# Gate and value products of a local feed-forward as three fp16 products, with the rows split on GpSimd

## The reference, cut to what matters

```python
def _layer(x, wqkv, qs, ksc, wo, lg, lb, w1, b1, w2, b2):
    ...
    x = x + o @ wo                              # window attention
    h = shift_token(x)
    mu = h.mean(-1, keepdims=True)
    var = h.var(-1, keepdims=True)
    h = (h - mu) / jnp.sqrt(var + 1e-05) * lg + lb
    h = h @ w1 + b1                             # 128 -> 2 * 341
    a, g = jnp.split(h, 2, axis=-1)
    h = a * jax.nn.gelu(g, approximate=False)
    x = x + h @ w2 + b2                         # 341 -> 128
    return x
```

## Time and profile before

| | |
|---|---|
| median of three executions | 1896.26 us |
| the profiled execution's own time | 1897.1 us |
| its span, first to last instruction | 1895.3 us |
| TensorE busy | 1763.1 us (93%) |
| VectorE, ScalarE, GpSimd busy | 1410.3, 1421.3, 1426.8 us (74 to 75%) |
| mean granted TensorE clock | 0.963 |
| local layers, first transpose to last write of x | 1300.1 to 1706.5 us |

### The profile page before, as it was taken

One profiled execution on the slowest core, in us unless ns is written; L12 is line 12 of the kernel. 1 busy time (PEld: TensorE's weight loads), 2 busy tenths in 40 slices (PEclk: granted clock), 3 DMA queues, 4 the chain that ended last, 5 costly groups with the idle time before them and its releaser, 6 DMA issues. The chain is left out here.

```text
span 1895.3 us, 54354 instructions
## 1 busy us (share of the span) xinstructions
PE 1763.1 (93%) x23048; PEld 1115.2 (59%) x23048; DVE 1410.3 (74%) x2595; ACT 1421.3 (75%) x1784; POOL 1426.8 (75%) x846
## 2 busy tenths in 40 slices
PE   5999999999999999999999999885999999977997
PEld 1466666666666666666666666582556666642454
DVE  5778878788787878878787776226988888824785
ACT  1688888888888888888888889814888888833463
POOL 3599899999999998998999999974755566504122
PEclk8899999999999999999999999987999999977988
DMA  4101010010101011010110100051211111100000
GB/s 120 26 22 30 19 30 24 25 30 22 27 22 30 24 25 31 19 30 19 31 28 21 27 18 2 2 172 23 44 36 36 37 36 40 28 4 13 1 1 23
DMA packets 71082, 56.91 MB, mean 30 GB/s; under 512 B 29197, under 2 KB 64185, under 8 KB 70841
## 3 DMA queue, kind: packets, MB, share of 16 engines
q1 hardware_dynamic: 70840, 53.44, 11.1%
HBM read 14.54 MB, written 1.05 MB: 8 GB/s over the span
## 5 line engine op out<-in xcount | busy, mean ns | idle before, releaser
L294 POOL TENSOR_TENSOR ah_probs_lo<-ah_probs,ah_probs_hi 128x1024 f16<-128x1024 f32 x512 | 1075.1, 2134 | 106.4 <-ACT ah_probs L493 104.1
L550 DVE TENSOR_REDUCE ah_part_max<-ah_p_m 128x1 f32<-128x512 f32 x1024 | 667.4, 685 | 165.0 <-PE ah_p_m L358 155.7
L490 ACT ACTIVATE ah_probs_hi<-ah_p_s 128x1024 f16<-128x1024 f32 x512 | 529.0, 1033 | 182.7 <-PE ah_p_s L377 176.7
L493 ACT ACTIVATE ah_probs<-ah_p_s 128x1024 f32<-128x1024 f32 x512 | 529.9, 1035 | 0.0
L391 PE MATMUL ah_p_o<-ah_v_hi,ah_probs_hi 128*128 128x65 f16 x4096 | 470.7, 195 | 4.8 <-POOL ah_probs_lo L294 4.6
L393 PE MATMUL ah_p_o<-ah_v_lo,ah_probs_hi 128*128 128x64 f16 x4096 | 470.7, 193 | 0.0
L395 PE MATMUL ah_p_o<-ah_v_hi,ah_probs_lo 128*128 128x65 f16 x4096 | 470.5, 194 | 0.0
L391 PEld LDWEIGHTS ah_p_o<-ah_v_hi,ah_probs_hi 128*128 128x128 f16 x4096 | 383.2, 98 | 86.0 <-DVE a_attn L565 12.3
L393 PEld LDWEIGHTS ah_p_o<-ah_v_lo,ah_probs_hi 128*128 128x128 f16 x4096 | 378.5, 98 | 91.4
L358 PE MATMUL ah_p_m<-ah_k_hi_lo,ah_q_hi_twice 128*128 128x512 f16 x1024 | 394.0, 385 | 6.5 <-DVE ah_part_max L550 5.0
L376 PE MATMUL ah_p_s<-ah_q_hi_twice,ah_k_hi_lo 128*128 128x512 f16 x1024 | 388.7, 380 | 1.1 <-ACT ah_probs L493 0.9
(11 more groups left out here) (279 smaller groups left out, 3100.2 us busy)
## 6 DMA issues: line engine op xcount, KB each, us to landing
ba_v_skew<-ba_v_own SPq DMA_DIRECT2D x64, 129.0 KB, 2.3
ah_q_hi_twice<-ah_hi SPq DMA_DIRECT2D x128, 64.0 KB, 2.0
ah_k_hi_lo<-ah_hi SPq DMA_DIRECT2D x64, 64.0 KB, 1.9
ah_one_k_hi<-ah_hi SPq DMA_DIRECT2D x64, 64.0 KB, 2.0
ah_k_hi_lo<-ah_lo SPq DMA_DIRECT2D x64, 64.0 KB, 2.0
ah_max_q_lo<-ah_lo SPq DMA_DIRECT2D x64, 64.0 KB, 2.0
ah_w_head<-in_w_heads SPq DMA_DIRECT2D x16, 160.0 KB, 2.4
bw_rot<-in_rot SPq DMA_DIRECT2D x4, 512.0 KB, 9.5
```

What stands on the lines that cost most here:

```text
L294: pool.tensor_tensor(pl[:, p % RW, :, :], pb[:, p % RP, :, :], ph[:, p % RW, :, :], ALU.subtract).then_inc(lo_pool, 1)
L490: act.activation(ph[:, p % RW, :, :], p_s[:, p % 2, :, :], ACT.Exp, scale=HD ** -0.5)
L493: act.activation(pb[:, p % RP, :, :], p_s[:, p % 2, :, :], ACT.Exp, scale=HD ** -0.5).then_inc(exp_done, 1)
L550: dve.tensor_reduce(part[:, t, 2 * half + b:2 * half + b + 1], p_m[:, b, :], AX, ALU.max).then_inc(maxed, 1)
```

## The change

The gate and value products, one fp32 product each, become three fp16 products: high weights by high rows, low weights by high rows, high weights by low rows, summed in PSUM. The high part is the fp16 value, the low part the fp16 value of the rest.

The weights `w1` are split on GpSimd in `prepare`, after the rotation tables, from a float32 buffer that now, like that of `wqkv`, is taken by a method `stage` inside `mha_out` and given back at its end. The loads of `w1` have a semaphore of their own.

The rows are split on GpSimd in `local_layers`: in step j, behind the clamp and ahead of the low probabilities, tile u = j-7 of `hT2` is cast to `hT2h` and the rest written to `hT2l`. `hT2` shrinks to two tiles of 128 columns. Gate chunk 0 waits for `hT2l_done` of four tiles in place of `hT2_done`; VectorE's write of `hT2` waits for the split two tiles back in place of `a_ready`.

```diff
@@ mha_out
         aT = sc.sb("attnT", [P, 2, IC, P])
+        local.stage(sc)
@@ LocalWeights
-        self.wqkv = sc.sb("wqkv", [P, DEPTH, 3 * INNER])
...
-        self.w1 = sc.sb("w1", [P, DEPTH, 2 * hid])
+        self.w1h = sc.sb("w1_hi", [P, DEPTH, 2 * hid], F16)
+        self.w1l = sc.sb("w1_lo", [P, DEPTH, 2 * hid], F16)
...
+    def stage(self, sc):
+
+        self.wqkv = sc.sb("wqkv", [P, DEPTH, 3 * INNER])
+        self.w1 = sc.sb("w1", [P, DEPTH, 2 * self.hid])
@@ prepare
+        pool.wait_ge(self.w1_in, 16 * DEPTH)
+        pool.tensor_copy(self.w1h[:, :, :], self.w1[:, :, :]).then_inc(self.w1_hi_done, 1)
+        pool.wait_ge(self.w1_hi_done, 1)
+        pool.tensor_tensor(self.w1l[:, :, :], self.w1[:, :, :], self.w1h[:, :, :],
+                           ALU.subtract).then_inc(self.w1_split, 1)
@@ local_layers, GpSimd, after the clamp
+                    u = j - 7
+                    if on(u):
+                        m, i = divmod(u, GROUP)
+                        ts = slice(i * P, (i + 1) * P)
+                        pool.wait_ge(hT2_done, u + 1)
+                        if m >= 2:
+                            pool.wait_ge(a_ready, HC * (m - 1))
+                        pool.tensor_copy(hT2h[:, m % 2, ts], hT2[:, u % 2, :]).then_inc(hT2h_done, 1)
+                        pool.wait_ge(hT2h_done, u + 1)
+                        pool.tensor_tensor(hT2l[:, m % 2, ts], hT2[:, u % 2, :], hT2h[:, m % 2, ts],
+                                           ALU.subtract).then_inc(hT2l_done, 1)
@@ local_layers, TensorE, gate
-                        pe.wait_ge(hT2_done, GROUP * (m + 1))
+                        pe.wait_ge(hT2l_done, GROUP * (m + 1))
...
-                    pe.matmul(p_h[0:n, :], lw.w1[:, l, col:col + n], hT2[:, m % 2, :], start=True,
+                    cs = slice(col, col + n)
+                    pe.matmul(p_h[0:n, :], lw.w1h[:, l, cs], hT2h[:, m % 2, :], start=True, stop=False)
+                    pe.matmul(p_h[0:n, :], lw.w1l[:, l, cs], hT2h[:, m % 2, :], start=False, stop=False)
+                    pe.matmul(p_h[0:n, :], lw.w1h[:, l, cs], hT2l[:, m % 2, :], start=False,
                               stop=True).then_inc(g_ready if which == 0 else a_ready, 1)
@@ local_layers, VectorE, h2T
-                        if m >= 2:
-                            dve.wait_ge(a_ready, HC * (m - 1))
-                        dve.tensor_scalar(hT2[:, m % 2, i * P:(i + 1) * P], p_e[:, P:2 * P], lw.gb[:, l, 0:1],
+                        if u >= 2:
+                            dve.wait_ge(hT2l_done, u - 1)
+                        dve.tensor_scalar(hT2[:, u % 2, :], p_e[:, P:2 * P], lw.gb[:, l, 0:1],
```

More of the change, by code:

```diff
@@ L802, in __init__ @@
         self.ff_in = sc.long_sem("ff_in")
-        self.FF = 16 * DEPTH * (4 + hc)
+        self.FF = 16 * DEPTH * (3 + hc)
+        self.w1_in, self.w1_hi_done, self.w1_split = (sc.long_sem(n) for n in ("w1_in", "w1_hi_done", "w1_split"))
+    def stage(self, sc):
+        self.wqkv = sc.sb("wqkv", [P, DEPTH, 3 * INNER])
+        self.w1 = sc.sb("w1", [P, DEPTH, 2 * self.hid])
     def prepare(self, pool):
@@ L840, in start @@
             sp.dma_start(self.gb[:, l, :], a["ln_gb"][l]).then_inc(self.ff_in, 16)
-            sp.dma_start(self.w1[:, l, :], a["w1"][l]).then_inc(self.ff_in, 16)
+            sp.dma_start(self.w1[:, l, :], a["w1"][l]).then_inc(self.w1_in, 16)
             sp.dma_start(self.b1[:, l, :, :], a["b1"][l]).then_inc(self.ff_in, 16)
@@ L886, in local_layers @@
         mv = sc.sb("mean_var", [P, RH, 2])
-        hT2 = sc.sb("h2T", [P, 2, CH])
+        hT2 = sc.sb("h2T", [P, 2, P])
+        hT2h = sc.sb("h2T_hi", [P, 2, CH], F16)
+        hT2l = sc.sb("h2T_lo", [P, 2, CH], F16)
         g_sb = sc.sb("gate", [P, HC, CH])
@@ L901, in local_layers @@
          h2n_done, h2_turned, hT2_done, g_ready, g_copied, gelu_done, a_ready, hid_done, d_ready, base_done,
-         xo_done) = (sc.sem(n) for n in (
+         xo_done, hT2h_done, hT2l_done) = (sc.sem(n) for n in (
              "consts", "cleared", "hT_turned", "hTh_done", "hTl_done", "q_ready", "k_ready",
@@ L908, in local_layers @@
              "h2n_done", "h2_turned", "hT2_done", "g_ready", "g_copied", "gelu_done", "a_ready", "hid_done",
-             "d_ready", "base_done", "xo_done"))
+             "d_ready", "base_done", "xo_done", "hT2h_done", "hT2l_done"))
         h_in = [sc.sem(f"h_in{b}") for b in range(2)]
@@ L1188, in _ @@
                         pe.wait_ge(lw.ff_in, lw.FF)
+                        pe.wait_ge(lw.w1_split, 1)
                     feed(j, 0)
```

## The result

Four executions of the changed kernel took 1907.13 to 1914.35 us, median 1910.17; four of the kernel before took 1893.14 to 1896.61, median 1896.01. The ratio is 1.0079, with an interval of 1.0057 to 1.0101: the change costs 14 us. The profiled execution of the changed kernel is its fastest, 1907.13 us with a span of 1905.3, so it stands 3.0 under its median.

The account below looks back on a forecast made before the run. TensorE is busy 93% of the span, but ScalarE ends the gate-product step and VectorE's hidden block gates the value step. Terms 14.5 - 3.5 + 6 - 1 = +16 us make 1912 us, range 1902 to 1921.

Parts of the forecast that it names:

- The place: GpSimd's split behind rotation sums and clamp: gate product 0 stops 3.63 us, ScalarE's copy 0 3.0 late; +14.5 us with savings.
- r=1: Feed-forward step with three value products: shorter products save 0.26 us a group; where TensorE's rate falls, -1 us in all.
- The stop at full rate: Gate-product steps of six groups, TensorE's rate unchanged: 6 x 2.76 - 0.5 = +16.1 us.
- The clock: TensorE's rate falls after the stop in most gate-product steps: 1.0 us for each of six, +6 us (0 to +9).
- The drain: Last two groups, attention drained: cheaper gate and value products, group 7's split hidden, group 6 paying 0.2 us; sum -3.5 us.
- The split and the weights: GpSimd: cast and subtraction of rows 291 and 427 ns; splitting w1 4.1 us, hidden in 13.65 us idle before layernorm.
- The sum: Whole kernel: 14.5 - 3.5 + 6 - 1 = +16 us, 1912 us against the median; chance 0.50.
- The clock that holds: Gate product 0 stops but TensorE keeps its full rate: +11 us, 1907 us; chance 0.27.
- a rate that stays low: TensorE's rate falls and stays low into the value and w2 product steps: +24 us, 1920 us; chance 0.12.
- The third: GpSimd splits the fourth tile before its rotation sums, gate product 0 on time: only 7 us of savings, 1889; chance 0.05.
- That the shift is taken in elsewhere: ScalarE's delay is absorbed elsewhere and the savings make up for it: within 0.2%; chance 0.03.
- Products that save nothing: Three fp16 gate or value products take as long as the fp32 pair: 7 us of savings go, +23, 1919; chance 0.03.

Follow-up runs that it names:

- the clock held by filling: The changed kernel with idle fp16 products on TensorE ahead of gate product 0's wait, in all six groups beside attention: 1902.94 us, ratio 1.0042.
- the repeat: The changed kernel run again unchanged, on the same chip as the kernel with idle products: 1913.67 us, ratio 1.0095.
- the run with the wait alone: The kernel before, fp32 products kept, with only the rows' split on GpSimd and gate product 0's wait for it added: 1922.24 us, ratio 1.0138.
- Both runs: The changed kernel with the rows' split on VectorE: high part by copy, 1919.94 us; high part by a second scaling out of PSUM, 1913.75 us.

## Why the prediction was right, step by step

**The place.** This was the main step, and it held: TensorE idle 3.50 us in group 2 (3.63 predicted), copy 0 late by 3.01 (3.0), the last idle time of ScalarE 1.00 in place of 1.24 (0.24 less), r=1 at 13.83 (0.25 less, 0.26 predicted). Two further places of the same block moved the time by -22 and +17 us from 1910.

**The stop at full rate.** Predicted 6 x 2.76 - 0.5 = +16.1 in r=0; with the clock held by filling, 87.16 - 71.46 = +15.7. Group 0's smaller share holds as well: 14.09 against 14.59.

**The clock.** Predicted +6 (0 to 9). In r=0 the changed kernel's own profile gives 92.33 - 87.16 = 5.2 and the repeat's 7.5. The granted clock was 0.79 to 0.89 in the five r=0 steps of groups 1 to 5 and 1.00 in group 0 in the first; in the repeat group 0 fell too (15.90 us at 0.79). That the rate falls "in most r=0 steps" is shown; in group 2 the step lost 15.54 - 14.59 = 0.95, where 1.0 was put. One detail held in part: gate 0 was to issue in 1.3 us at the lower level. Where the rate fell during the stop it did (1.25 and 1.26 us in groups 1 and 3, 1.23 to 1.26 in four groups of the repeat); where it fell behind the stop gate 0 issued in 0.66 to 0.85 us, and the loss came in the transposes. The sentence drawn from the Trainium skill, "TensorE: Matmul & The Clock Gate", Part 1, that idle time brings the throttled state back, agrees with these runs: with the idle time filled the fall did not come. How long a stop must be the runs don't settle, and the prediction's nearest row, 2.55 us, was a fair guess and no rule. Group 0's stop of 3.08 us left the clock at 1.00 in one profile of the changed kernel and was followed by the lower level in the other. In the drain of the first, 2.85 us without work were followed by products 0.22 apart in group 6 and 0.40 to 0.43 apart in group 7.

**r=1.** Predicted -1.6 for the value products and -1 where the rate falls; measured -2.2 together, with 14.50 in place of 14.84 in group 3, where the rate fell in both. The sum has other parts than predicted: group 0 gives 1.1 of it (14.89 to 13.80), because the rate fell there before (0.89) and not after, groups 1, 2 and 4 give the 0.25 of the shorter product, and group 5 nothing (12.80 and 12.79).

**The drain.** Predicted -3.5; -3.1 here, and between -1.2 and -3.8 over the seven profiles of the six kernels with the new products and GpSimd's split. Its length goes with the granted clock in it: 46.50 to 47.20 us at 0.82, 47.7 at 0.79, 48.6 and 49.1 at 0.72. The kernel before had 50.27 at 0.80, so at the nearest clock the products are worth 2.5 to 2.6. One detail was the other way round: group 7's gate did wait for the split (1.37 us, against 1.19 for the write of x), and group 6's did not.

**The split and the weights.** Groups of instructions on GpSimd in the changed kernel (busy us, mean ns | idle before):

```profile
L1021 POOL TENSOR_TENSOR ba_h2T_lo<-ba_h2T,ba_h2T_hi 128x128 f16<-128x128 f32 x32 | 13.7, 427 | 2.7
L1019 POOL CAST ba_h2T_hi<-ba_h2T 128x128 f16<-128x128 f32 x32 | 9.3, 292 | 9.2 <-DVE ba_h2T L1470 9.2
L835 POOL TENSOR_TENSOR bw_w_lo<-ao_w,bw_w_hi 128x1364 f16<-128x1364 f32 x1 | 2.8, 2781 | 0.1
L130 POOL TENSOR_SCALAR g_x<-ao_rows,g_ln_mean_var,g_ln_rstd 128x128 f32<-128x128 f32 x3 | 2.8, 924 | 10.0 <-DVE g_ln_rstd L117 10.0
L833 POOL CAST bw_w_hi<-ao_w 128x1364 f16<-128x1364 f32 x1 | 1.3, 1318 | 0.0
```

The line through two lengths gave 291 and 427 ns for the split; 292 and 427 were measured. The weights' 4.1 us went into the idle time ahead of the layernorm, which shrank from 13.65 to 10.0 us.

**The sum.** In the profile the terms make 20.9 - 2.2 - 3.1 = +15.6 (+16 predicted), and the span grew by 10.1. The other 5.6 us came off in code that the change leaves alone: 3.0 behind the layers, 1.2 in the steps ahead of the feed-forward, 1.1 from the first transpose to those, 0.3 before. In the first three of these stretches the granted clock was higher in this execution (0.92 against 0.89, 1.00 against 0.98, 0.75 against 0.69). The stretch behind the layers, as windows of the kernel before and of the changed one:

```profile
1706.55:1895.29 188.74, 156.25 (x552) 85.72 (x552) 121.22 (x245) 87.65 (x153) 53.08 (x78) 0.89 0.03 9
1719.61:1905.35 185.74, 152.76 (x552) 82.74 (x552) 121.08 (x245) 87.63 (x153) 53.04 (x78) 0.92 0.03 10
```

Over the eleven profiles it took 185.7 to 185.9 us at 0.92 (six), 188.7 to 189.2 at 0.89 (four) and 187.2 at 0.91 (one). The changed kernel itself had 185.74 in the first profile and 189.06 in the repeat, so it is not the change; what decides it no run shows. Against the median the change costs 14.2, and in the repeat 18.5 (1913.67 against 1895.17). That the forecast lies 2 us from the first of these is in part luck; that r=0 grew by 20.9 and 23.2, where 16.1 + 6 was put, is not.

**The rivals.** The clock that holds (1907) and a rate that stays low (1920) are out: the first by the r=0 windows, the second by r=2 at 9.59 (its terms, 14.5 - 3.5 + 9 + 6, also make 26 and not the 24 stated). The third, gate 0 on time, didn't come with this order of the code; it was priced at 1889, and the kernel with the split ahead of the sums took 1888.18. That the shift is taken in elsewhere is out by copy 0's row. Products that save nothing are out by the run with the wait alone, 9 to 12 us above the changed kernel. That is more than the 7 us of savings priced, and most of it lies in r=0 (100.20 us for six there, 92.33 and 94.67 in the two profiles of the changed kernel): behind the stop an fp32 gate 0 issues in 1.41 to 1.87 us (1.79 on average over the six), the new one in 0.64 to 1.26 (0.86, and 1.08 in the repeat).

## What to carry to other kernels

A short helper instruction on an engine that runs in order can cost what stands ahead of it, not its own length: look up when its input is ready, what its engine does at that moment, and put it into the idle time ahead of the long work. Count with a stop of a pipelined TensorE twice, once for the stop and once for the clock behind it (here 2.65 and 0.9 to 1.25 us a group). When a wait goes, look at what its engine waits for next: moving one copy ahead of a table load was worth another 5 us.

## What was not expected of the hardware

VectorE was held up by GpSimd. A 128x128 copy from SBUF to SBUF took 1.50 to 1.63 us beside GpSimd's 1.90 us product and 0.23 alone; a subtraction of two SBUF operands of that size 1.18 to 1.31 us beside it and 0.29 alone, and 0.44 to 0.45 beside a short GpSimd sum of 0.45; reading PSUM, 0.40 beside it. Each held instruction ended 0.08 to 0.15 us after GpSimd's. The Trainium skill, "SBUF — State Buffer", section "Who interferes with whom", says that VectorE and GpSimd share a pair of ports as an exclusive lock, and that copies and casts of VectorE in a two-port mode and its operations with two SBUF inputs contend for it. Both runs agree in what was held up and what was not; in which mode the copy ran no row shows.
